# Masked attention: mask products as four 64x64 tiles, and one cut of the transposed scores less

## The reference, cut to what matters

```python
energy = jnp.einsum('nqhd,nkhd->nhqk', q, k)                  # 16 heads of 16 columns
energy = jnp.where(mask == 0, jnp.float32(-1e+20), energy)    # one 128 x 128 mask for all
attn = jax.nn.softmax(energy / jnp.sqrt(jnp.float32(embed)), axis=3)
out = jnp.einsum('nhql,nlhd->nqhd', attn, v).reshape(n, q_len, embed)
out = out @ Wo.T + bo
```

## Time and profile before

| | us |
|---|---|
| median of three runs | 3878.18 |
| lowest and highest run | 3874.96, 3878.55 |
| span of the profiled execution, first to last instruction | 3869.9 |
| TensorE busy | 3678.2 |
| VectorE busy | 3088.5 |
| ScalarE busy | 2207.4 |
| GpSimd busy | 2200.5 |

### The profile page before, as it was taken

One profiled execution on the slowest core, in us unless ns is written; L12 is line 12 of the kernel. 1 busy time (PEld: TensorE's weight loads), 2 busy tenths in 40 slices (PEclk: granted clock), 3 DMA queues, 4 the chain that ended last, 5 costly groups with the idle time before them and its releaser, 6 DMA issues. The chain is left out here.

```text
span 3869.9 us, 134428 instructions
## 1 busy us (share of the span) xinstructions
PE 3678.2 (95%) x47408; PEld 2870.0 (74%) x47408; DVE 3088.5 (80%) x5266; ACT 2207.4 (57%) x4529; POOL 2200.5 (57%) x3316
## 2 busy tenths in 40 slices
PE   5999999995799999999999996999999999999999
PEld 4777777773688888888888884566666668888888
DVE  4888888885778777778777775798888977777777
ACT  3777777775444444444444442577677765555554
POOL 5666666664245443333333334466666667887777
PEclk9999999997899999999999998899999999999999
DMA  4677777774332322222222224799999952232322
GB/s 130 197 204 207 214 209 209 205 213 154 102 85 79 84 68 74 66 70 69 68 72 68 72 66 90 158 211 216 211 217 208 215 151 80 75 77 75 79 75 72
DMA packets 834241, 502.59 MB, mean 130 GB/s; under 512 B 262037, under 2 KB 824408, under 8 KB 833480
## 3 DMA queue, kind: packets, MB, share of 16 engines
q1 hardware_dynamic: 832680, 493.49, 50.5%
q0 software_dynamic: 928, 0.49, 0.1%
HBM read 251.27 MB, written 214.96 MB: 120 GB/s over the span
## 5 line engine op out<-in xcount | busy, mean ns | idle before, releaser
L1556 ACT ACTIVATE phase_spare<-phase_loop_hid,phase_b1T 128x128 f32<-128x128 f32 x2048 | 586.1, 368 | 710.9 <-PE phase_loop_hid L193 702.2
L1129 DVE TENSOR_REDUCE phase_loop_mx<-phase_loop_score 128x8 f32<-128x1024 f32 x512 | 625.4, 1222 | 98.5 <-PE phase_loop_score L882 91.0
L1522 PE MATMUL phase_loop_moe_y<-phase_w,phase_spare 128*128 x2048 | 693.6, 379 | 0.1
L1037 ACT ACTIVATE phase_loop_pt<-phase_loop_scoreT 128x1024 f32<-128x1024 f32 x448 | 458.6, 1024 | 268.3 <-PE phase_loop_scoreT L916 265.8
L1524 PE MATMUL phase_loop_moe_y<-phase_w,phase_spare 128*128 x2048 | 558.2, 273 | 0.0
L191 PE MATMUL phase_loop_hid<-phase_loop_moe_h,all_w_first_hi 128*128 128x128 f16 x2048 | 449.2, 219 | 0.0
L192 PE MATMUL phase_loop_hid<-phase_loop_moe_h,all_w_first_hi 128*128 128x128 f16 x2048 | 449.1, 219 | 0.0
L192 PE MATMUL phase_loop_hid<-phase_loop_moe_h,phase_w_hi 128*128 128x128 f16 x2048 | 449.1, 219 | 0.0
L193 PE MATMUL phase_loop_hid<-phase_loop_moe_h,all_w_first_lo 128*128 128x128 f16 x2048 | 449.1, 219 | 0.0
L193 PE MATMUL phase_loop_hid<-phase_loop_moe_h,phase_w_lo 128*128 128x128 f16 x2048 | 449.1, 219 | 0.0
L191 PE MATMUL phase_loop_hid<-phase_loop_moe_h,phase_w_hi 128*128 128x128 f16 x2048 | 449.0, 219 | 0.0
(11 more groups left out here) (293 smaller groups left out, 11038.9 us busy)
## 6 DMA issues: line engine op xcount, KB each, us to landing
qk_scratch<-phase_loop_qk SPq DMA_DIRECT2D x192, 256.0 KB, 3.4
phase_loop_cin<-in_ctx SPq DMA_DIRECT2D x128, 256.0 KB, 4.6
x_scratch<-phase_loop_x SPq DMA_DIRECT2D x128, 256.0 KB, 3.1
h_scratch<-phase_loop_hr SPq DMA_DIRECT2D x128, 256.0 KB, 3.7
phase_loop_qS<-qk_scratch SPq DMA_DIRECT2D x384, 64.0 KB, 2.8
phase_loop_kS<-qk_scratch SPq DMA_DIRECT2D x384, 64.0 KB, 2.4
ks_scratch<-ct_scratch SPq DMA_DIRECT2D x384, 64.0 KB, 2.4
all_w_first_lo<-ks_scratch SPq DMA_DIRECT2D x128, 192.0 KB, 4.0
```

Of the source, the lines that this page charges most:

```text
L1037: act.activation(pt[n % len(pt)][:, :, :], score_t_bank[:, :].rearrange("p (j n) -> p j n", j=HB2), ACT.Exp, scale=exp_scale).then_inc(s_e ...
L1129: v.tensor_reduce(to, score_bank[:, :].rearrange("p (h j n) -> p h j n", h=2, j=CH), AX.X, ALU.max).then_inc(s_mx.sem, 1)
L1522: pe.matmul(o[:, :], hh[n % NH][:, j, :], row, start=half == 0 and j == 0, stop=False, skip_group_check=True)
L1556: i = act.activation(hf[n % NF][:, j, :], hid(u, n)[:, j * S:(j + 1) * S], ACT.Gelu, bias=w["b1"][:, bass.ds(e * HB + (4 * half + j), 1)], ...
```

## The change

All mask products are made by `mask_tiles`: in place of two products of the full array, four of 64x64 tiles. The first two take rows 0 to 63 and 64 to 127 of the mask to the same output rows of the first bank. The other two take rows 0 to 63 of the array to output rows 64 to 127 of the second bank, and rows 64 to 127 to output rows 0 to 63. For these the mask must lie with its halves exchanged, so there are second masks, `mask_x` and `maskT_x`, made by four transfers on GpSimd's queue in the preparation. Part 1 of the transposed scores gets a `mask_score_t(1)` on TensorE, just ahead of `score_t(1)`; the cut on VectorE, its `keep_min` and its place in VectorE's list are gone. Part 3 is left with GpSimd.

```diff
--- before.py
+++ after.py
@@ -55,10 +55,9 @@
 M_X = 15
 AHEAD, SPLIT_AHEAD = 4, 8
 NEXT_DEPTH, NEXT_START = 5, dict(zip(("sync", "tensor", "scalar", "gpsimd", "vector"), (5, 5, 5, 5, 6)))
-KEPT = 3e38
 
 LOOP = 4
-CUT_BY_MIN, CUT_BY_PRODUCT = (1,), (3,)
+CUT_BY_PRODUCT = (3,)
 
 
 def p2(e):
@@ -508,7 +507,7 @@
         m3 = two("m3", [P, PAIR, P], F16)
         mT = two("mT", [P, PAIR, S], F16)
         pt = (two if first else four)("pt", [P, HB2, S], F32)
-        cut_by = () if first else CUT_BY_MIN + CUT_BY_PRODUCT
+        cut_by = () if first else CUT_BY_PRODUCT
         yE = two("yE", [P, PAIR, 512], F32)
         rec = two("rec", [P, PAIR, HEADS], F32)
         yn = two("yn", [P, PAIR, D], F32)
@@ -576,16 +575,11 @@
 
         def cut(eng, n):
 
-            with_min = n in CUT_BY_MIN
-
             def go(u):
-                if with_min:
-                    s_e.wait(eng, u, n + 1)
-                else:
-                    s_x[n].wait(eng, u)
-                keep, op = (w["keep_min"], ALU.min) if with_min else (w["keep"], ALU.mult)
+                s_x[n].wait(eng, u)
                 p_n = pt[n][:, :, :]
-                eng.tensor_tensor(p_n, p_n, keep[:, :].unsqueeze(1).to_broadcast([P, HB2, S]), op).then_inc(s_cut[n].sem, 1)
+                eng.tensor_tensor(p_n, p_n, w["keep"][:, :].unsqueeze(1).to_broadcast([P, HB2, S]),
+                                  ALU.mult).then_inc(s_cut[n].sem, 1)
             return go
 
         def ahead_of(u, count):
@@ -884,13 +878,19 @@
                         m.then_inc(s_s.sem, 1)
                     return go
 
+                def mask_tiles(bank, rows, crossed):
+
+                    for b, part in enumerate((rows, crossed)):
+                        for i in range(2):
+                            k_at, out_at = slice(64 * i, 64 * i + 64), slice(64 * (i ^ b), 64 * (i ^ b) + 64)
+                            pe.matmul(bank[out_at, b * 512:(b + 1) * 512], c["identb"][k_at, k_at], part[k_at, :],
+                                      start=True, stop=False, skip_group_check=True)
+
                 def mask_score(n):
 
                     def go(u):
                         s_mx.wait(pe, u, n)
-                        for hh in range(2):
-                            pe.matmul(score_bank[:, hh * 512:(hh + 1) * 512], c["identb"][:, :], w["mask"][:, :], start=True,
-                                      stop=False, skip_group_check=True)
+                        mask_tiles(score_bank, w["mask"], w["mask_x"])
                     return go
 
                 def t_max(u):
@@ -922,9 +922,7 @@
 
                     def go(u):
                         s_e.wait(pe, u, n)
-                        for hh in range(2):
-                            pe.matmul(score_t_bank[:, hh * 512:(hh + 1) * 512], c["identb"][:, :], w["maskT"][:, :],
-                                      start=True, stop=False, skip_group_check=True)
+                        mask_tiles(score_t_bank, w["maskT"], w["maskT_x"])
                     return go
 
                 def av(n):
@@ -980,7 +978,7 @@
                              (6, av(1)), (4, score(2))]
                 else:
                     tasks = [(6, av(0)), (3, score(0)), (8, make["t_y"]), (5, mask_score_t(0)), (4, make["t_max"]),
-                             (5, score_t(0)), (3, mask_score(1)), (6, av(1)), (3, score(1)), (5, score_t(1)),
+                             (5, score_t(0)), (3, mask_score(1)), (6, av(1)), (3, score(1)), (5, mask_score_t(1)), (5, score_t(1)),
                              (1, make["q"]), (7, make["y1"]), (3, mask_score(2)), (5, mask_score_t(2)), (3, score(2)),
                              (6, av(2)), (5, score_t(2)), (6, av(3)), (3, mask_score(3)), (6, make["y0"]),
                              (3, score(3)), (5, score_t(3)), (8, make["o"]), (2, mask_score(0))]
@@ -1030,7 +1028,7 @@
                     def go(u):
                         s_st.wait(act, u, n + 1)
                         s_av.wait(act, u, n + 1 - len(pt))
-                        if n in cut_by and n in CUT_BY_PRODUCT:
+                        if n in cut_by:
                             act.activation(pt[n][:, :, :], score_t_bank[:, :].rearrange("p (j n) -> p j n", j=HB2),
                                            ACT.Relu, scale=-exp_scale).then_inc(s_e.sem, 1)
                             return
@@ -1150,7 +1148,7 @@
                              (1, lo_c), (8, norm1_stats), (6, low_ahead)]
                 else:
                     tasks = [(8, norm_y(0)), (10, add_x), (4, row_max(0)), (10, norm1_stats), (9, lo_y),
-                             (4, row_max(1)), (8, norm_y(1)), (2, lo_q), (4, row_max(2)), (6, cut(v, 1)),
+                             (4, row_max(1)), (8, norm_y(1)), (2, lo_q), (4, row_max(2)),
                              (4, row_max(3))]
                 run_steps(v, tasks, units, DEPTH, **follow("vector", v))
 
@@ -1656,7 +1654,7 @@
     return {"wa": (k.sb("wa_hi", [P, 1, P], F16), k.sb("wa_lo", [P, 1, P], F16)),
             "wo": (k.sb("wo2_hi", [P, KB, D], F16), k.sb("wo2_lo", [P, KB, D], F16)),
             "mask": k.sb("mask4", [P, CH * S], BF16), "maskT": k.sb("maskT4", [P, CH * S], BF16),
-            "keep": k.sb("keep", [P, S], F32), "keep_min": k.sb("keep_min", [P, S], F32), "valid": k.sb("valid", [P, PAIR], F32),
+            "keep": k.sb("keep", [P, S], F32), "mask_x": k.sb("mask4x", [P, CH * S], BF16), "maskT_x": k.sb("maskT4x", [P, CH * S], BF16), "valid": k.sb("valid", [P, PAIR], F32),
             "bo_b": k.sb("bo_b", [P, D], F32)}
 
 
@@ -1670,7 +1668,8 @@
     mi = kk.sb("mask_int", [P, S], I32)
     kept, away = kk.sb("mask_kept", [P, S], F32), kk.sb("mask_away", [P, PAIR], F32)
     b1, b2, b3, b4 = (kk.ps(f"sh_ps{i}") for i in range(4))
-    s_z, s_ld, s_mk, s_pe, s_v, s_a, s_row = (kk.sem(f"sh_{x}") for x in ("z", "ld", "mk", "pe", "v", "a", "row"))
+    s_z, s_ld, s_mk, s_pe, s_v, s_a, s_row, s_turned, s_cross = (
+        kk.sem(f"sh_{x}") for x in ("z", "ld", "mk", "pe", "v", "a", "row", "turned", "cross"))
 
     def gpsimd(g):
         for t in bd:
@@ -1683,6 +1682,16 @@
             for h in range(P // DK):
                 at = slice(h * DK, (h + 1) * DK)
                 g.dma_start(t[at, at], io[f"L1_xattn_{name}"]).then_inc(s_ld, 16)
+
+        def cross(to, given):
+
+            g.dma_start(to[0:64, :], given[64:128, :]).then_inc(s_cross, 16)
+            g.dma_start(to[64:128, :], given[0:64, :]).then_inc(s_cross, 16)
+        g.wait_ge(s_v, 1 + CH)
+        cross(w["mask_x"], w["mask"])
+        g.wait_ge(s_turned, CH)
+        cross(w["maskT_x"], w["maskT"])
+        g.wait_ge(s_cross, 64)
 
     def tensor(pe):
         pe.wait_ge(s_ld, 16 * (3 * (P // DK) + 2))
@@ -1727,9 +1736,8 @@
                                in1=w["wo"][0][:, :, :], op0=ALU.mult, op1=ALU.subtract)
         v.wait_ge(s_pe, 4)
         for j in range(CH):
-            v.tensor_copy(w["maskT"][:, j * S:(j + 1) * S], b4[:, 0:S // 2].bitcast(BF16))
+            v.tensor_copy(w["maskT"][:, j * S:(j + 1) * S], b4[:, 0:S // 2].bitcast(BF16)).then_inc(s_turned, 1)
         v.tensor_scalar(w["keep"][:, :], b4[:, 0:S // 2].bitcast(BF16), 0.0, None, ALU.is_equal)
-        v.tensor_scalar(w["keep_min"][:, :], b4[:, 0:S // 2].bitcast(BF16), 0.0, KEPT, ALU.is_equal, ALU.mult)
 
     return {"tensor": tensor, "scalar": scalar, "vector": vector, "gpsimd": gpsimd}
```

## The result

The changed kernel takes 3886.6 us (median of 7 runs, 3876.28 to 3893.36), the kernel before 3874.96 us in the same comparison (7 runs, 3873.43 to 3878.55). The ratio is 1.0024, 95% interval [1.0013, 1.0036]: slower by 0.24%, where 3868 us and a gain were forecast.

What follows compares the result with a forecast made beforehand. TensorE was taken to bound the masked attention: -0.44 us its own, +0.14 and +0.06 from other engines, so -0.24 a unit, 15 us over 64, less 5 for the placing: span 3860 us, median 3868; range 3850 to 3902.

Steps and rivals of the forecast that it cites:

- The tiles and their price: Mask products on TensorE: a group of four tiles takes 0.23 us, each change of tiling costs 0.09 to 0.10 us.
- rounds: Rival, mask products: tiles of a group run in two or three rounds, 3944 or 4042 us; chance 0.07 together.
- dearer 64x64 changes in general: Rival, TensorE: changes into or out of 64x64 tiling cost 0.05 to 0.08 us more each, 3901 to 3924 us; chance 0.13.
- free ones: Rival, TensorE: changes between 64x64 and 64-row tiles cost nothing, 0.3 us less a unit, 3850 to 3856 us; chance 0.08.
- TensorE's own sum, -0.44: TensorE's work per masked-attention unit: -1.26 + 0.23 + 0.70 - 0.11 = -0.44 us, before waits for other engines.
- two of them replace a loss that is there now: Two of seven added tiling changes, ahead of mask products behind f32 transpositions, replace an existing loss: -0.11 us a unit.
- What the other engines take back: Waits of TensorE per unit: +0.14 us at `t_max` for the maxima, +0.06 at `av(2)` for `copy_y(0)`, leaving -0.24.
- (5) The placing: Maxima going through SyncE's queue to memory and back before `score_t(0)`: late more often, taking three tenths of the gain, 5 us.
- The preparation: Four mask transfers on GpSimd's queue, hidden behind the block's last instructions: counted as nothing, about 1 us once without that cover.
- +8.3 us around the span: Whole kernel: the median of the runs lies 8.3 us above the profiled span, so 3860 us becomes 3868.
- The likeliest case (0.50): Whole kernel: the result as summed, a gain, 3858 to 3873 us; chance 0.50.
- the gain is given back: Rival: circles of other engines, the placing first, hold the step where it is, 3874 to 3882 us; chance 0.22.

Runs made afterwards that it cites:

- again: The changed kernel itself, unaltered, compared a second time with the kernel before: 3885.85 us, ratio 1.0035.
- copy_between_lo: The changed kernel with `copy_y(0)` between `expo(0)` and `expo(1)` on ScalarE and `row_max(2)` ahead of `lo_q` on VectorE: 3885.36 us, ratio 1.0018 to the kernel before.
- prep_only: The kernel before with only the four transfers of the exchanged masks added in the preparation, unused: 3875.41 us, ratio 1.0003.
- cut_only: The changed kernel with full-array pairs, seven of them, in place of the tiles: 3899.29 us, ratio 1.0065 to the kernel before.
- copy_between: The changed kernel with `copy_y(0)` moved on ScalarE to between `expo(0)` and `expo(1)`: 3884.45 us, ratio 1.0013 to the kernel before.

## Why the prediction was wrong

- **The tiles and their price** were right in the main. A group costs 0.24 us (0.23 predicted), 0.01 us of it between its two rows; a change of tiling costs 0.10 (0.09 to 0.10). The rivals of rounds, of dearer 64x64 changes in general and of free ones fell. (Of changes between 64x64 and 64-row tiles there are four in a unit, not three: `score_t(0)` to `mask_score(1)` is one as well. Each costs about what the others do.) The Trainium skill's sentence in "TensorEngine Tiling (Array Packing)", "Restrictions and Gotchas", on different row tiles and one PSUM bank doesn't hold here for the bank as a whole: both row tiles write one bank, on different partitions, and start within 0.01 us. The Trainium skill's drain at a change of mode, in the same page's "Key Properties", agrees with the trace, at 0.10 us a change.
- **"TensorE's own sum, -0.44"** was too good by about 0.17. Taking the holes out of 11.41 leaves 11.09 us, which is -0.27. The seven groups are 0.05 to 0.07 of it. "y0" to `score(3)` takes 0.59 us where it took 0.53: I had priced the new change ahead of "y0" on the group before it, and nothing on the transpositions themselves. And of the -0.11 us for "two of them replace a loss that is there now" half failed: "y1" to `mask_score(2)` takes 0.53, as that gives, but `t_y` to `mask_score_t(0)` takes 0.59 in place of 0.54, the change on top of the loss.
- **"What the other engines take back"** is the step that failed: it counts the circle of `av(2)` and leaves out the one through VectorE that holds the same stretch. I gave +0.14 for the maxima and +0.06 for `av(2)`; the rows show 0.08, 0.17 and 0.07. For `av(2)` the circle was right and the handing over too small: `copy_y(0)` ends 2.11 us after "q" starts (3055.26; 2.10 predicted), but `av(2)` starts 0.15 us after that end, not 0.04. The third circle, "y1", `norm_y(1)`, `lo_q`, `row_max(2)`, `mask_score(3)`, isn't in the prediction. It could have been: all its links stand in the trace of before, 3.14 us to the end of `row_max(2)` and 0.06 to hand over, so about 3.20. There TensorE took 3.28 us for the stretch, which by my own terms was to shrink to 2.90; in the changed kernel the chain takes 3.14. I had looked at VectorE's cut, between `row_max(2)` and `row_max(3)`, and taken the freed 1.69 us for room. Sum: -0.27 + 0.32 = +0.05 in place of -0.24. Put by stretches of the step, this circle is 0.18 of the 0.29 us by which the step missed ("y1" to `mask_score(3)`, 3.14 us where 2.90 + 0.06 were forecast), and 0.07 are in `mask_score(3)` to `score(3)` (0.93 where 0.97 - 0.21 + 0.10 were). What else TensorE's own sum lacks lies mostly in the stretch that the maxima hold anyway.
- **(5) The placing** was put at 3/10 of the gain. With no gain there was nothing for it to take, and the waits went from 11.8 us to 7.2 (12.5 in `again`). Where the circles were opened it took more than was said: in `copy_between_lo` the waits are 23.6 us, 12 more than before (8 more than in `prep_only`), and 64 steps of 11.17 in place of 11.36 us would bring 12.
- **The rest of the loss.** 64 x 0.05 = 3 us. From the last `t_max` to the end of the span it is 719.9 us in place of 717.9, and 719.4 in `again`: 1.5 to 2.0 us. `cut_only`, with seven products but no tiles, takes 718.8, so about 0.9 goes with the seventh product, which stands alone in the drain; in the changed kernel a stretch of 3.4 us at the lower clock lies there besides, at 3182 us, which neither before nor `cut_only` has. The preparation wasn't free: the first load behind it is issued 1.0 us after VectorE's last instruction, before 0.3, so 0.7 us. That makes 6 of the 9 to 13 us. The other 3 to 7 fit late units that cost more for the clock (4 low stretches in `again`, 1 before, at 1.4 us each), but that sum is argued, not shown. In the trace of `again`, 9.7 us longer than that of before, 6.5 us lie between the first and the last `t_max`, of which the step is 3.3.
- **+8.3 us around the span** was wrong as a reading: the changed kernel's profiled run took 3876.28 us at a span of 3874.5, so 1.8 us lie around it, and the profiled execution of before was a quick one. The difference between the two kernels isn't touched by it.
- The likeliest case (0.50) and the sign were wrong. The rival "the gain is given back" had the right outcome, a step held where it was, but put the placing and SyncE's queue first, which didn't hold it, and ended at 3882 us, 4.6 short of what came. That 3886.6 lies within 3850 to 3902 is owed to the width of the range, which was made for the dearer changes of tiling; no case of the prediction gives this number.

## What to carry to other kernels

Where an order written by hand runs without holes, every circle of the other engines that is just long enough is invisible: write down each one that begins and ends on the bound engine, with its length and the bound engine's own time for the same stretch after the change, before counting a gain. An operation's freed time on another engine helps only the circle it is in; here the circle that held was one operation earlier. And test an opened circle by whether its hole closes or moves: `copy_between` moved 0.17 us from one product to another and the step stayed the same to 0.01 us.

## What the runs showed of the hardware

- Four 64x64 tiles of 512 bf16 columns, two by two into each of two banks, run side by side in 0.24 us, where one full-array product of 512 columns costs 0.22: four tiles do in one such time what the pair did in two.
- Four f32 transpositions cost 0.59 us from start to start when they stand between 64x64 tiles and 48-row products, in either order, where they cost 0.49 and 0.53 with a full-array product in place of the tiles.
- In the kernel before the clock stayed at 1.00 behind all 15 forced waits, 1.2 us long in the mean; with seven full-array pairs it fell twice. In the changed kernel, with 16 of 1.3 us in the mean, it fell to 0.50 seven times, for 3.4 or 6.8 us. Over all traces, waits of 1.3 to 1.6 us were followed by a fall in 3 of 15 cases with full-array mask products and in 10 of 22 with tiles. A fall adds about 1.4 us, so a faster way to do the same work can make a wait dearer.
